# Graph network on one Trainium2 core: double-buffered step inputs, first-phase totals transposed by VectorE, another order of totals and taps in the layers

## The reference

```
w = silu(silu(edge_attr_8 @ W1 + b1) @ W2 + b2) @ W3 + b3       # 4 blocks of 8x8 per edge
hs, hv = h[src, :8], h[src, 8:].reshape(-1, 8, 3)
m0 = ALPHA * (hs*sh0 . w00 + INV_SQRT3 * (hv . sh1) . w110)
m1 = ALPHA * (hs . w01 * sh1 + hv*sh0 . w10)
x = layernorm(x + h_self + segment_sum(messages, dst, 12500) / sqrt(16))
for each of three layers (bn: batch norm, leaky: leaky relu, none in the third):
    z = einsum('nc,kco->nko', x, W)                              # 64 taps
    msg = sum over 8 corners s of basis[:, s] * z[src, wi[:, s]]
    x = bn(leaky(segment_sum(msg, dst) / count + x @ R + b) + x)
x = layernorm(x1 + x)                                            # x1: the input of the layers
```

## Time and profile before

| | us |
|---|---|
| median of 3 runs | 20935.47 |
| the three runs | 20923.95 to 20955.69 |
| the profiled execution | 20972.87 |
| its span | 20971.1 |

### The profile page before, as it was taken

How to read it: one execution, slowest core, us unless ns; L and a number is a source line. 1 busy time by engine, 2 the same in 40 slices (tenths; PEclk the granted TensorE clock), 3 DMA queues, 4 the chain that set the end, 5 groups by cost and what they waited for, 6 DMA issues and landing times.

```text
span 20971.1 us, 186425 instructions
## 1 busy us (share of the span) xinstructions
PE 15345.2 (73%) x56679; PEld 8301.8 (40%) x56679; DVE 11311.1 (54%) x19047; ACT 3317.7 (16%) x4009; POOL 11415.3 (54%) x12003
## 2 busy tenths in 40 slices
PE   7788888888866767677766767676766667677766
PEld 3333334333334444344433444444443444344433
DVE  5555556555555555555555555555555555555555
ACT  1111111111111111111111111111111111111111
POOL 4455555555545555555545555555554555555554
PEclk7666766666678888888888888888888888888888
DMA  1000000000010000000010000000001000000001
GB/s 33 13 14 15 15 14 15 15 14 14 14 23 16 16 16 16 16 16 16 16 24 16 16 16 16 16 16 16 16 16 23 16 16 16 16 16 16 16 16 23
DMA packets 977322, 353.01 MB, mean 17 GB/s; under 512 B 701603, under 2 KB 968820, under 8 KB 977012
## 3 DMA queue, kind: packets, MB, share of 16 engines
q0 software_dynamic: 386208, 210.78, 5.8%
q1 hardware_dynamic: 385724, 112.32, 2.4%
q10 hardware_dynamic: 205336, 29.28, 0.9%
HBM read 314.88 MB, written 36.56 MB: 17 GB/s over the span
## 4 chain that ended last, share of the span: by engine, by line
PE 51%; another core or an unknown queue 28%; issue 11%; ACT 4%; DVE 4%; ACTq 1%; DMA 0%; POOL 0%; DVEq 0%; SPq 0%; POOLq 0%
PE ps L1504 17%; PE ps L1516 17%; PE ps L1412 6%; PE ps L1527 4%; PE ps L1428 3%; ACT big L753 3%; PE ps L1401 2%; PE ps L1395 2%; DVE big L1009 1%; ACTq L760 1%; PE ps L1385 0%; ACT big L677 0%; ACT rts L654 0%; PE ps L1364 0%
## 5 line engine op out<-in xcount | busy, mean ns | idle before, releaser
L540 POOL DMA_INDIRECT xg<-x_rows,idx x8790 | 8335.9, 948 | 6314.6 <-DVE big L1203 3725.6
L1504 PE MATMUL ps<-big 128*128 128x256 f32 x18816 | 5106.6, 425 | 1190.3 <-ACT big L753 1146.3
L1186 DVE TENSOR_TENSOR big<-ps,onehot 128x1024 f32<-128x1024 f32 x2352 | 2865.7, 1218 | 5162.1 <-remote 3480.6
L1504 PEld LDWEIGHTS ps<-big 128*128 128x128 f32 x18816 | 3903.7, 213 | 3062.8 <-issue 2517.7
L540 POOL DMA_INDIRECT xg<-in_x,idx x3125 | 2989.8, 957 | 2901.8 <-issue 1863.9
L1527 PE MATMUL ps<-big,w_taps 128*32 128x512 f32 x9408 | 1576.2, 748 | 3107.3 <-issue 3075.5
L753 ACT COPY big<-ps 128x1024 f32<-128x1024 f32 x2352 | 2350.4, 1013 | 8764.1 <-PE ps L1504 5510.2
L1516 PE MATMUL ps<-xw,row_hot 128*128 128x512 f32 x8232 | 3670.7, 597 | 16.7 <-DVE picked L1195 10.7
L1412 PE MATMUL ps<-w,big 65*128 65x256 f32 x6272 | 2438.3, 529 | 182.7 <-DVE big L1009 168.5
L1516 PEld LDWEIGHTS ps<-xw,row_hot 128*128 128x128 f32 x8232 | 1544.1, 190 | 1970.6 <-issue 1945.2
L1412 PEld LDWEIGHTS ps<-w,big 65*128 65x128 f32 x6272 | 1520.8, 260 | 1903.7 <-issue 1531.2
(11 more groups left out here) (139 smaller groups left out, 6760.1 us busy)
## 6 DMA issues: line engine op xcount, KB each, us to landing
xg<-x_rows,idx POOLq DMA_INDIRECT x8790
xg<-in_x,idx POOLq DMA_INDIRECT x3125
row_of<-pick_rows SPq DMA_DIRECT2D x294, 128.0 KB
agg_rows<-rts ACTq DMA_DIRECT2D x294, 64.0 KB
meta<-in_coord_t SPq DMA_DIRECT2D x294, 48.0 KB
idx<-in_src_t SPq DMA_DIRECT2D x784, 8.0 KB
big<-in_rad SPq DMA_DIRECT2D x196, 64.0 KB
meta<-meta_items SPq DMA_DIRECT2D x392, 32.0 KB
```

Of the source, the lines that this page charges most:

```text
L540: return nc.gpsimd.indirect_dma_start(out=dst_tile, out_offset=None, in_=table, in_offset=bass.IndirectOffsetOnAxis(ap=index, axis=0))
L1186: v.tensor_tensor(bm[:, ring], hat_outer[:, its].rearrange("p n c b -> p n (c b)").unsqueeze(3) .to_broadcast([P, 4, 16, J]), onehot[:, it ...
L1504: tr = nc.tensor.matmul(ps[:, 2 * (ch % 2) + r // 2, 256 * (r % 2):256 * (r % 2) + 256], xm[:, at].rearrange("p a c -> p (a c)"), bm[:, at ...
```

## The change

1. `idx`, `meta`, `carry`, `xg` and `row_of` get two buffers, by the parity of the step, with semaphores by parity; the loops of SP, POOL and VectorE go by pairs of steps. The indices of a step come by one load of 32 columns. The gathers of a step wait for the use of the quarter two steps back. Those of steps 0 and 1 of each phase wait for no use. At a layer's start SP issues the loads of its first two steps ahead of the stores of the nodes. `row_hot` and `picked` move into the shared tile `big`.
2. In the first phase TensorE's eight products per step and ScalarE's copy of 64x264 go. VectorE transposes R into `rts` (`turn_first`), right behind the scan. ScalarE stores the sums with a DMA of 64 pieces of 1 KB, copies the 32x16 degrees and stores them with a second DMA. A row of `first_rows` is laid out in two halves, each 256 sums and 8 degrees.
3. In a layer TensorE's totals stand behind chunk 4 in place of chunk 3, the taps in pairs behind chunks 6 and 7 in place of one behind each of chunks 4 to 7, and ScalarE's copy and store of the totals ahead of its copy of chunk 6 in place of chunk 4.

```diff
@@ tiles
-        idx = sb("idx", [P, STEP], I32)
-        meta = sb("meta", [P, META, STEP])
-        carry = sb("carry", [P, STEP])
-        xg = sb("xg", [P, STEP, CH])
+        idx = sb("idx", [P, 2, STEP], I32)
+        meta = sb("meta", [P, 2, META, STEP])
+        carry = sb("carry", [P, 2, STEP])
+        xg = sb("xg", [P, 2, STEP, CH])
...
@@ SP: one layer's loads
+            def layer_loads(l, i, par, twice):
+
+                early = isinstance(i, int) and i < 2
+                load_indices(l + 1, i, par, twice)
+                load_meta(i, par, (l + 1) * STEPS if early else (l + 1) * STEPS + i - 1, coord_table, 0, 3)
+                load_picks(i, par, PK * l * STEPS if early else PK * (l * STEPS + i - 1))
...
                 for i in range(2):
-                    load_meta(base + i, i, coord_table, 0, 3)
-                    load_indices(i, lambda q: rows_in(path, q, l + 1, i))
-                    load_picks(l * STEPS + i, i)
...
+                    layer_loads(l, i, i, 0)
+                store_nodes(x_rows, x_ready, WB * l, x_stored)
...
@@ POOL: a layer
-                gather_sources(x_rows, (l + 1) * STEPS,
-                               lambda q: pool.wait_ge(xm_ready[2 * q + 1], l * STEPS) if l else None,
-                               picked_in=path.picks)
...
+                def layer_gathers(i, par, twice):
+
+                    last = isinstance(i, int) and i == STEPS - 1
+                    free = (None if isinstance(i, int) and i < 2
+                            else lambda q: (xm_ready[2 * q + 1], l * STEPS + i - 1))
+                    gather_sources(x_rows, l + 1, par, twice, free, padded if last else STEP, path.picks)
...
@@ ACT: the rows of the first phase
             def l0_rows(i):
-                store_rows(i, slice(64, P), 8 * CELL0, 7, 16 * i)
-                act.dma_start(cells_at(first_rows, i, 2), rts[64:P, :].rearrange("p (q f) -> p q f", q=8)
+                act.wait_ge(rt_out, i + 1)
+                to = first_rows[ds(i * STEP, STEP), :].rearrange("i (h f) -> i h f", h=2)
+                act.dma_start(to[:, :, 0:HALF_F], rts[0:CH, 0:ROW].rearrange("p (h f) -> p h f", h=2)
                               ).then_inc(rows_stored, 16)
+                deg = rts[CH:2 * CH, ROW:ROW0]
+                nc.scalar.copy(deg, rts[CH:2 * CH, 0:ROW].rearrange("p (s c) -> p s c", c=CH)[:, :, 0]
+                               ).then_inc(deg_out, 1)
+                act.wait_ge(deg_out, i + 1)
+                act.dma_start(to[:, :, HALF_F:HALF0], deg.rearrange("p (h s) -> p h s", h=2)).then_inc(rows_stored, 16)
...
@@ ACT: a layer's step
-                    if ch == 4 and with_rows:
+                    if ch == 6 and with_rows:
                         l1_rows(l, i - 2)
...
@@ DVE
+            def turn_first(n):
+
+                dve.wait_ge(R_ready, n + 1)
+                if due(n):
+                    dve.wait_ge(rows_stored, 32 * n)
+                v.transpose(rts[0:2 * CH, 0:ROW], R[0:2 * CH].rearrange("p s i -> p (s i)")).then_inc(rt_out, 1)
...
@@ PE
                 l0_degrees(i)
-                if with_totals:
-                    totals_by_cell(i - 1, True)
...
-                    if with_totals and ch == 3:
-                        totals_by_cell((l + 1) * STEPS + i - 2, False)
-                    if with_taps and ch >= 4:
-                        tap_products(l, i - 1, 1 - par, ch - 4)
+                    if with_totals and ch == 4:
+                        totals_by_cell((l + 1) * STEPS + i - 2)
+                    if with_taps and ch >= 6:
+                        for t in (2 * ch - 12, 2 * ch - 11):
+                            tap_products(l, i - 1, 1 - par, t)
```

More of the change, by code:

```diff
@@ L317, in rows_in, with loads, whole_pairs @@
             mine = [QUART * q + r for r in range(QUART) if not (phase and q in path.picks and r == PICK)]
[L318 to L321 removed]
+            whole = 2 * steps_of(path, par)
+            earlier = rows_in(path, par, q, phase - 1, whole)
+            if isinstance(twice, int) and twice == whole:
+                padding = sum(s >= last_tiles(path) for s in mine) if (path.steps - 1) % 2 == par else 0
+                return earlier + 8 * len(mine) * whole - 16 * padding
+            return earlier + 8 * len(mine) * twice
+        def loads(path, par, phase, twice):
+            return 16 * phase * steps_of(path, par) + 8 * twice
+        def whole_pairs(begin, end):
+            return begin + 2 * ((end - begin) // 2)
         def pairs_end(path):
@@ L908, in vector_program, with scan @@
             SCAN = 3
-            def scan(n, at, parts):
+            def scan(n, at, parts, phase, par, twice):
                 own = slice(0, parts)
@@ L1140, in l1_step @@
                 if path.picks:
-                    dve.wait_ge(row_loaded, 16 * (n1 + 1))
+                    dve.wait_ge(row_loaded[par], loads(path, par, l, twice))
                     if due(n1):
```

347 lines of the change are left out of this document (178 added, 169 removed).

## The result

The changed kernel took 20967.15 us (median of 20 runs, 20919.07 to 21021.2), the kernel before 20913.97 (20 runs, 20863.15 to 20984.51): a ratio of 1.0026, 95% interval [1.0017, 1.0035], some 54 us slower. The forecast was 83 us faster. The profiled executions (20972.87 before, 20954.6 after) lie the other way round by 18 us; each is one execution out of a spread of over 100 us, so the pair shows where time moved, and its sign is not the result's.

A forecast was written before the change was run, and what follows sets the result against it. It took unbroken GpSimd gathers delaying TensorE's results as the layers' bound. Terms +76 (layers), +78, +17, -9 (starts, ends), -245 (first phase) sum to -83 us: 20,890 profiled, 20,852 as median; range 20,450 to 21,250.

The forecast's parts named there:

- a ring of run, release and third piece: Layer step: gathers back to back 27.2 us, wait after them 4.1, work to the next gather 19.05; together 50.3.
- some 8 us or more into a run: Layers: TensorE results coming that far into unbroken gathers wait for their end and about 4 us more.
- -245 + 17: First phase: 245 us gained in its steps, 17 us lost by 32 more gathers at its start.
- its 59: Sign for the first phase: 57.8 us a step expected; over 59 makes the forecast wrong.
- 49 to 50.7: Sign for the layers: 49.9 us a step expected; under 49 or over 50.7 makes the forecast wrong.
- The first phase, -245 us: First phase: TensorE's saved 1.33 us and 1.2 us from results taken up earlier, together -2.5 us in 98 steps.
- promptness: First phase: with less TensorE work ahead, more results come before gathers delay them; 1.2 us per step, two thirds of 1.74.
- The layers, +76 us: Layers: the new order of totals, copy and taps costs 0.26 us a step in 294 steps.
- four steps in five cold and one in five warm: Layers: TensorE at half clock for the first taps in four steps of five, +0.6 us; full clock otherwise, -1.1.
- in the middle of the run: Layers: chunk 4's result comes out there, in the totals' former place; chunk 5 and the totals are held to the end.
- cold taps: Rival, layers: both tap pairs at half clock, chunk 7 half so; +1.5 us a step, +441 us, 21,217 us; chance 0.25.
- Starts and ends, +86 us: Phase starts and ends: more gathers at starts, less at ends +78, first phase +17, earlier index loads -9.

The follow-up runs named there:

- gate: Kernel before plus two waits in GpSimd's layer program, for ScalarE's copies of chunks 4 and 6, ahead of the third and fourth quarters of gathers: 21,975 us, 1.0453 (late results).
- totals_only: Kernel before with only part 2 of the change, the first phase's totals by VectorE's transpose: 20,484 us, 0.9921 of before (late results).
- no_ahead_b: Changed kernel, but gathers wait for the use of the step just before, as in the kernel before: 20,734 us, 1.0044 of before (late results).
- after_c: Changed kernel unedited, once more, on the same chip as some of its parts: 20,763 us, 1.0061 of the kernel before (late results).
- after_again: Changed kernel unedited, run again beside the kernel before on another chip with late results: 20,781 us, 1.0137 of before.
- after: Recorded profile of the changed kernel, unedited: profiled execution 20954.6 us, median of its runs 20967.15 us.
- the second chip: Chip with late results where both kernels ran again unedited: kernel before 20,477 us, changed kernel 20,781 us, 1.0137.

## Why the prediction was wrong

- **What bounds the kernel.** Right: results of TensorE held back by a run of gathers, a ring of run, release and third piece. Not seen, and not to be seen in one trace: that it depends on the chip (or the hour). On the other kind GpSimd's issue is the bound. The "some 8 us or more into a run" holds for the ring of these kernels only: in gate a result was held that ended 6.75 us into a run.
- **The recorded miss.** Forecast -83, measured +54. By the profiled pair (-18) the failed step is the first phase's: with its start it gave -65 where -245 + 17 was forecast, so 163 us were missing. The starts and ends of the layers came to +30 for +69 (32 and 49 at the starts, 42 back in the last steps, 9 at the end), and the other steps of the layers to +11 for +76, which made up for part of it. Of the signs that the prediction named, a first-phase step of 59.6 us is over its 59; the layer step of 49.4 is inside 49 to 50.7. On the other chips with late results the layers' term failed too.
- **The first phase, -245 us.** This step failed wherever it was measured with late results. totals_only gives 163. If all of TensorE's 1.33 us a step came, then 0.3 of the 1.2 for promptness did; the two weren't told apart. The transpose cost what the product row said (0.70 for 0.675). That it was hidden is likely, not shown. Within the whole change the steps of the first phase behind the first give -105 us in the recorded pair and -24 in the second. Part of the rest goes with part 1 of the change (58.85 us a step in no_ahead_b, 58.04 in totals_only), and the lookahead isn't to blame: with it a step takes 58.25 (after_c). The cause is open.
- **The layers, +76 us.** This step failed on three chips, the other way in the recorded pair. The order alone costs 0.9% on one, 207 us by the medians (21,234.75 less 21,027.99), and the layers' steps cost 229 us with the whole change on another and 241 from totals_only to no_ahead_b on the third. Two assumptions failed. One is "four steps in five cold and one in five warm" for the new order. The short third piece of the kernel before (16.6 us) comes from taps 0, chunk 5 and taps 1, which TensorE does on the totals' copy just ahead of the release. The change takes just that work from there and puts it behind the release. It could be read in the trace before: at 8091.01 taps 0 stand in the run, behind the totals' copy. The other is that chunk 4 comes out "in the middle of the run": in 5 to 27% of the rings of the whole change (after_c, after_again, after) it came at the run's end. The rival "cold taps" had the picture (3.88 us for the first pair and 2.9 for chunk 7 forecast, 3.64 and 2.91 measured, the second pair at full clock in both) and at +1.5 us per step too high a price, for 0.8 to 1.0 measured. I gave it 0.25.
- **Clock.** The rule of the Trainium skill that I cited ("TensorE: Matmul & The Clock Gate", Part 1) agrees: 1.56 us of idle and 1.97 us for chunk 6 in one ring, 7.04 us of idle and taps at half clock (3.64 us for two groups) in the other. By that rule the slower side deserved more than it got.
- **Starts and ends, +86 us.** Right in sign and about in size in the profiles. The starts take 41, 32, 29 and 19 us in the recorded pair, 9 come back at the end and 42 in the last steps of the layers: some +70. On the second chip it is 36, 32, 29 and 6, with 13 and 33 back: +58. Against no_ahead_b it is less, 28 by the medians and 49 by the profiles, since there the lookahead also shortens the other steps of the first phase.
- **The sum.** Order +0.9%, totals -0.8%, lookahead +0.1 to 0.2%: +0.3% by the parts, which were measured on two chips. The whole change measured 1.0026, 1.0061 and 1.0137, so that the parts meet the first of these is in part luck: on the chip of the second, order and part 1 without its lookahead cost 1.2% together.

## What to carry to other kernels

Where a row waits for an unknown queue behind an engine that had long been done, look at what the software DMA queue issues at that time, and test with a pause in that queue before moving work about. An order of work is judged by what stands just ahead of the wait that ends last, not only by what stands behind it: what an engine can do while it would wait anyway is free, and here it kept TensorE's clock up as well (1.97 us and not 3.75 for the same eight products). And a gain of a per cent that was tuned on one chip should be run on several: here the same new order costs nothing on one kind of chip and 0.9% on the other, and the same pause is -12% or +18%.

## What the runs showed of the hardware

- The kernel before took 15.43 ms on two chips and 20.5 to 21.0 ms on three. What differs between them is open, as is whether it is the chip or the hour; the one chip that was measured twice took 20,498 and 20,921 us.
- On the three, TensorE's results reach ScalarE and VectorE late while GpSimd issues indirect DMAs of 128 rows every 1.25 us. In the run that starts at 8046.84 chunk 3 is still copied without such a wait, at 8055.52; chunk 4, whose products end at 8057.2, isn't until 8067.28. In gate a result that ended 6.75 us into the run was held already. Of the held ones one comes out in a run, at no fixed time (13.6, 20.4 and 24.7 us into it in the three rings shown, 11 to 30 over the recorded trace of the kernel before), the others when it ends, with the release 3.9 to 4.1 us after it on average with the old order.
- A gap of 0.8 us ahead of each four gathers brought a layer's step to 44.4 us, where VectorE waits for gathered rows; one ahead of each eight left it at 47.8.
- The rate of gathers was the same on both kinds, 1.25 us each.
